# Upper parts of rotated rows and of later pages made on GpSimd instead of ScalarE, in a fused attention and FFN kernel

## The chip, the cores and the metric

The kernel runs on one core of a Trainium2 chip. The core has five engines, each with an instruction queue of its own: TensorE (PE, matmuls), VectorE (DVE), ScalarE (ACT), GpSimd (POOL) and SyncE (SP), which only issues DMAs here. Engines meet through semaphores. The metric is the device time of the whole program in microseconds (us).

## The reference

The reference is one transformer block with layer norms after each half, for x of shape (4, 512, 1024):

```python
def attn(x, wq, wk, wv, wo):             # 32 heads of 32, 8 key and value heads
    q, k, v = x @ wq, x @ wk, x @ wv
    q, k = rope(q), rope(k)              # pairs of columns rotated by position
    scores = q @ k.T / sqrt(32) + causal_mask
    return (softmax(scores) @ v) @ wo    # each k and v head serves 4 q heads

x = layernorm(x + attn(x, wq, wk, wv, wo))
gate = x @ (gate_t * gate_s[:, None]).T  # gate_t, up_t, down_t hold -1, 0, 1
up = x @ (up_t * up_s[:, None]).T        # 3584 hidden columns
hidden = silu(gate) * up
x = layernorm(x + hidden @ (down_t * down_s[:, None]).T)
```

All is float32 from outside.

## The kernel before

**Numbers.** Float32 operands are cut into an upper and a lower float16 part, and a product is three float16 matmuls (upper by upper, upper by lower, lower by upper). Two kinds of such cuts matter here.

*Pages.* x (16 pages), wq (8), wkv (4) and wo (8) come in as 36 pages of 128 partitions by 1024 float32, one DMA each (`page_load`, on SP). The upper part is made by `split_hi`, an activation Copy with a scale on ScalarE (line 1241; the first three pages are cut in halves, line 1239). The lower part is made by `split_lo` on VectorE (line 1384): page times scale minus upper part. The first 12 pages (`NFIRST`) have a buffer each, laid over tiles that are not used yet; the other 24 go through two buffers, `page0` and `page1`, so that a load waits for the split of the page two before it. These 24 are four pages of wq, the eight of wo and the twelve of x of the later three batches. The split of such an x page also waits until the former batch's q projection has used the place that it writes.

*Rotated rows.* Each q or k projection of 128 rows by 8 heads lands in PSUM (line 1070). VectorE multiplies it with cosines and sines (`rotate`, lines 1403 and 1405), GpSimd adds the two (`rope_add`, line 1631), ScalarE writes the upper float16 part twice into `stack_rows` (`nat_hi`, line 1257, 512 elements per partition), GpSimd writes the lower part (`nat_lo`, line 1638), and a transposing DMA on SP puts it into `q_stack` or `k_stack` (`stack`). There are 64 such rows for q and 16 for k. Two buffers each serve the rotated sum and the stack rows, so a `rotate` waits for `nat_hi` and `nat_lo` of two rows before.

**Attention.** It goes by 16 units (a batch and 8 heads). For a unit, PE first forms the scores by rows (`score_q`, line 1086); VectorE takes their maxima (`row_max`, lines 1414 to 1420), ScalarE exponentiates and sums them (`row_sum`, line 1280), and a few small steps make maximum plus logarithm of the sum (`ln_seed`, `ln_step`, `max_parts`, `max_tr`, `max_copy`, `max_rows`), which becomes three more rows of `q_stack`. Then PE forms the scores again by keys (`score_k`, line 1111), ScalarE exponentiates them (`exp`, line 1266), GpSimd zeroes the upper triangle (`causal`, line 1645), and PE multiplies with v (`pv`, line 1127). ScalarE and VectorE take the result out as two parts (`att_hi`, `att_lo`) and a DMA spills it. Projections of later units and output projections with wo (also line 1070) fill PE between these. Finished rows are added to x (`residual`), normed (`norm_stats`, `newton` on GpSimd, `norm`) and spilled, also as sums and differences in float16 (`x1_form`, `x1_hi`, `x1_lo`, `xF_store`).

**FFN.** It uses a scheme of seven products for each two by two blocks (line 1170, `product`). Its right operands, x1_forms, come back from DRAM by transposing DMAs (`xF_load`, line 1760); they lie over the projection weights and may start only when the last q projection is done. Weight pages are loaded (`w_load`), turned from int32 into float16 on ScalarE (`w_cast`, line 1319) and combined on VectorE (`w_form`). The down products (`down`, lines 1195 and 1211) are added up on VectorE (`acc`, line 1601). It makes two passes over the weights.

**What sets the order.** Every piece of work is put into a `Plan` with an engine, a rank (roughly its due time), a duration in us and the pieces it comes after. `Plan.close` is a list schedule: it steps through planned time, and on each engine the ready piece of the lowest rank goes next. The outcome is one fixed order for each engine; the program then issues exactly that, with semaphore waits. `SHIFTS` (line 232) adds a number to the rank of each kind of piece on its engine: a larger one makes that kind give way to others. `AT_ONCE` names pairs of kinds on one engine where the planner assumes no delay between the end of one and the start of the next. Each engine works strictly in its order, so an instruction that waits holds up all behind it.

Of the kernel before, what the change touches and what calls it, by code (L numbers as in the profile page):

```python
# [10 lines left out]
ACT = mybir.ActivationFunctionType  # L11

P = 128
# [8 lines left out]
UH = 8  # L22
# [192 lines left out]
def room_after(n):  # L215

    p, r = divmod(n, NF)
    if r > 2:
# [13 lines left out]
SHIFTS = {  # L232
    PE: {"down": 20, "max_tr": 17, "product": 45, "proj_out": -9, "proj_q": 126, "pv": 12, "score_k": 5, "score_q": 13},
    SC: {"exp": 328, "hid_hi": -4, "ln_exp": 32, "nat_hi": 381, "norm": 21, "row_sum": 156, "silu": 43, "split_hi": 54,
         "v_copy": -17, "w_cast": 233, "x1_hi": 8, "x1_store": 1},
    VE: {"acc": 3, "add_x1": -55, "att_lo": 195, "bound": 21, "d_form": 40, "ds_scale": 6, "hid_form": 9, "hid_lo": 37,
         "hidden": 55, "ln_seed": -2, "ln_step": 43, "max_copy": 218, "max_parts": 9, "norm_stats": 76, "residual": -4,
         "rotate": -64, "row_max": 53, "split_lo": 31, "sum": 14, "w_form": 60, "x1_lo": 18},
    PO: {"nat_lo": 7, "newton": -12, "rope_add": -45, "scale_row": 11, "x1_form": -2},
    SY: {"att_load": -3, "att_store": 58, "bound_load": -34, "bound_store": -16, "d_in": -20, "d_store": 64, "ds_load": -20,  # L240
         "last_x1": -2, "max_rows": -14, "out_store": 11, "page_load": -4, "row_load": -4, "stack": 11, "w_in": -30, "w_load": 19,
         "w_store": -24, "xF_load": 130, "xF_store": 3},
}


AT_ONCE = {("sum", "hidden"), ("hidden", "hid_form"), ("hid_form", "hid_form"), ("ln_step", "max_parts"), ("d_form", "d_form"), 
           ("residual", "norm_stats"), ("acc", "norm_stats"), ("x1_form", "x1_form"), ("ln_seed", "ln_step"), ("norm", "x1_store")}

# [87 lines left out]
def attention_plan(plan):  # L336
# [17 lines left out]
    for n, (what, b, j) in enumerate(loads):  # L354
        at = ranks[what, b, j]
        before = n - 2 if n >= NFIRST + 2 else NFIRST - 1 if what == "wo" else -1
        last = [loads[n - 1]] if n else []
        put(SY, at, .4, "page_load", what, b, j, moves=2 * FIRST_MOVES if n == 0 else FIRST_MOVES if n < NFIRST else PAGE_MOVES,
            after=[("split_lo", *loads[before])] if before >= 0 else [])
        put(SC, at, .95, "split_hi", what, b, j, after=[("page_load", what, b, j)] + [("split_hi", *w) for w in last] + (  # L360
            [("proj", "q", UNITS * b - 1, j, KD - 1)] if what == "x" and b else []))
        put(VE, at, 1.14, "split_lo", what, b, j, after=[("split_hi", what, b, j)] + [("split_lo", *w) for w in last])
# [26 lines left out]
    for n, (at, long, (what, w, t)) in enumerate(groups):  # L389
# [29 lines left out]
        put(PO, end + 1, .68, "rope_add", *one, after=[("rotate", *one)])  # L419
        put(SC, end + 2, .53, "nat_hi", *one, after=[("rope_add", *one)] + ([("nat_hi", *one_back)] if r else []) + ([("stack", *two_back)] if r > 1 else []))  # L420
        put(PO, end + 3, .68, "nat_lo", *one, after=[("nat_hi", *one)] + ([("nat_lo", *one_back)] if r else []))
# [299 lines left out]
def block_kernel(nc, xT, x, wq, wkv, wo, gateT, upT, downT, gate_s, up_s, down_s,  # L721
# [18 lines left out]
    with ctx:  # L740
        def sem(name):
            return ctx.enter_context(nc.semaphore(name))
# [79 lines left out]
        s_page = [sem(f"page_dma{i}") for i in range(2)]  # L822
        s_hi, s_lo = sem("split_hi"), sem("split_lo")
        s_half_hi, s_half_lo = sem("first_half_hi"), sem("first_half_lo")
# [40 lines left out]
        rot_n = {w: n for n, (k, w) in enumerate([p for p in plan.order[VE] if p[0] == "rotate"])}  # L865
        for engine, kind in ((PO, "rope_add"), (SC, "nat_hi"), (PO, "nat_lo"), (SY, "stack")):
            assert [w for k, w in plan.order[engine] if k == kind] == list(rot_n), kind
        splits = [w for k, w in plan.order[SY] if k == "page_load"]
        split_n = {w: n for n, w in enumerate(splits)}
        for engine, kind in ((SC, "split_hi"), (VE, "split_lo")):  # L870
            assert [w for k, w in plan.order[engine] if k == kind] == splits, kind
        trans = [(k, w) for k, w in plan.order[PE] if k == "max_tr" or (k == "score_q" and row_bank(*w) == TRANS)]
# [343 lines left out]
        def scalar_program(e):  # L1216
            on = Waits(e)
            e.dma_start(tab[:, :, :, :], rope).then_inc(s_tab, 16)
            for kind, which in plan.order[SC]:
                if kind == "split_hi":  # L1220
                    n = split_n[which]
                    if n == NFIRST - 2:
                        e.dma_start(idH[:, :], identH).then_inc(s_const, 16)
                        e.dma_start(idB[:, :], identB).then_inc(s_const, 16)
                        e.dma_start(cmask[:, :], causal).then_inc(s_const, 16)
                    elif n == NFIRST + 2:
                        e.dma_start(sg[:, :], gate_s).then_inc(s_scale, 16)
                        e.dma_start(su[:, :], up_s).then_inc(s_scale, 16)
                    src, arrived, times = page_of(n)
                    on.wait_ge(arrived, 16 * times)  # L1230
                    if which[0] == "wo":
                        on.wait_ge(s_lo, NFIRST)
                    if which[0] == "x" and which[1]:
                        on.wait_ge(s_proj, proj_n["q", which[1] * UNITS - 1, which[2]] + 1)
                    up = X_UP if which[0] == "x" else W_UP
# [6 lines left out]
                elif kind == "v_copy":  # L1242
# [5 lines left out]
                                         scale=PROJ_DOWN).then_inc(s_v, 1)  # L1248
                elif kind == "nat_hi":
                    r = rot_n[which]  # L1250
                    on.wait_ge(s_add, r + 1)
                    on.wait_ge(s_set, 1)
                    on.wait_ge(s_stack[r % NNAT], 16 * (r // NNAT))
                    rows = nat[:, r % NNAT, :, 0:STK].rearrange("p h (f c) -> p h f c", f=3)
                    fields = slice(0, 3, 2) if which[0] == "k" else slice(0, 2)
                    ta = ropeA[:, r % NNAT, :].rearrange("p (h c) -> p h c", h=UH)
                    nc.scalar.activation(rows[:, :, fields, :], ta.unsqueeze(2).broadcast_to([P, UH, 2, HD]),
                                         ACT.Copy).then_inc(s_nhi, 1)
                elif kind == "exp":
# [102 lines left out]
        def vector_program(e):  # L1362
# [7 lines left out]
            for kind, which in plan.order[VE]:  # L1370
                if kind == "split_lo":
# [5 lines left out]
                    if n < HALVED:  # L1377
# [4 lines left out]
                        hi, lo, whole = hi[:, mid:], lo[:, mid:], whole[:, mid:]  # L1382
                    on.wait_ge(s_hi, n + 1)
                    nc.vector.scalar_tensor_tensor(lo, whole, up, hi, ALU.mult, ALU.subtract).then_inc(s_lo, 1)
# [237 lines left out]
        def gpsimd_program(e):  # L1622
            on = Waits(e)
            nc.gpsimd.memset(nat[:, :, :, STK:P], MAX_ONE).then_inc(s_set, 1)
            for kind, which in plan.order[PO]:
                if kind == "rope_add":
# [3 lines left out]
                    to = ropeA[:, r % NNAT, :]  # L1630
                    nc.gpsimd.tensor_tensor(to, to, ropeB[:, r % 2, :], ALU.add).then_inc(s_add, 1)
                elif kind == "nat_lo":
                    r = rot_n[which]
# [49 lines left out]
        def sync_program(e):  # L1683
            on = Waits(e)
            for kind, which in plan.order[SY]:
                if kind == "page_load":
                    n = split_n[which]
                    dst, arrived, times = page_of(n)
                    if n >= NFIRST + 2:
                        on.wait_ge(s_hi, n - 1)  # L1690
                        on.wait_ge(s_lo, n - 1)
# [187 lines left out]
```

## Time and profile before

| what | us |
|---|---|
| median of 3 runs | 1781.22 |
| lowest and highest run | 1777.97 and 1781.43 |
| the profiled execution, its own time | 1779.99 |
| its span from first to last instruction | 1778.2 |

The profile is of one execution. Busy times are sums over an engine's instructions, in us of the span. PE has 9456 matmuls; they are pipelined and their ends are modelled, so small gaps between them can hide in its busy time. The chain of waits goes back from the last instruction, at each step to what released it, and gives each line its share of the stretch. The stage up to about 690 us is attention with its projections, the rest the FFN. TensorE's granted clock is 0.995 of full speed over the span.

### The profile page before, as it was taken

What the parts mean: (1) busy time and instruction counts of PE and PEld (TensorE: products, weight loads), DVE (VectorE), ACT (ScalarE), POOL (GpSimd) and SP (SyncE); (2) the same over time, 40 slices, a digit from 0 to 9 for tenths busy, and PEclk for the clock granted to TensorE, in tenths of its full rate; (3) what the DMA queues carried; (4) which work ended last, traced back from release to release, by engine and by line L of the source; (5) the groups of instructions that cost most, each with busy time, mean ns of one, the idle gap of its engine ahead of it and who ended that gap; (6) DMA issues with size and microseconds to landing.
All of it is one profiled execution on the core that took longest, in us unless ns stands there. A gap on an engine that the chain in (4) does not pass through costs nothing.

```text
span 1778.2 us, 26642 instructions
## 1 busy us (share of the span) xinstructions
PE 1711.6 (96%) x9456; PEld 824.8 (46%) x9456; DVE 1208.3 (68%) x2593; ACT 967.4 (54%) x2201; POOL 409.1 (23%) x782
## 2 busy tenths in 40 slices
PE   7979999999999999999999999999999999999998
PEld 4634555555455434444444444444444444443444
DVE  7776668478667744677877768746667666678456
ACT  6799989789978874472553543531323233231321
POOL 3324445445434442410000002103100000003113
PEclk9999999999999999999999999999999999999999
DMA  8543345335235698582653545658312112133202
GB/s 266 104 141 61 70 114 144 61 96 155 56 67 138 163 222 297 170 300 95 207 173 130 202 159 194 219 146 195 115 60 87 42 65 86 42 110 106 96 13 83
DMA packets 228004, 233.44 MB, mean 131 GB/s; under 512 B 183200, under 2 KB 183840, under 8 KB 227872
## 3 DMA queue, kind: packets, MB, share of 16 engines
q1 hardware_dynamic: 224704, 222.86, 42.9%
q10 hardware_dynamic: 3168, 8.88, 1.3%
q8 instruction: 75, 1.23, 0.3%
q14 instruction: 57, 0.47, 0.1%
HBM read 122.78 MB, written 72.88 MB: 110 GB/s over the span
## 4 chain that ended last, share of the span: by engine, by line
PE 71%; DVE 9%; DMA 8%; ACT 8%; issue 2%; POOL 1%; SPq 1%; DVEq 0%; ACTq 0%; POOLq 0%
PE bank L1170 31%; PE bank L1070 13%; PE bank L1211 12%; PE bank L1195 6%; ACT bank L1280 3%; PE bank L1111 3%; PE bank L1127 3%; PE bank L1086 2%; DMA w_page<-gateT 2%; DMA x_forms<-x_forms_spill 1%; ACT p_tiles L1266 1%; DMA w_page<-upT 1%; DMA q_stack<-max_rows 1%; DMA x_forms_spill<-x_parts 1%; DVE acc L1620 1%
## 5 line engine op out<-in xcount | busy, mean ns | idle before, releaser
L1170 PE MATMUL bank<-x_forms,weight_forms 128*128 128x512 f16 x3136 | 705.0, 379 | 7.8 <-DVE up_blocks L1566 4.1
L1170 PEld LDWEIGHTS bank<-x_forms,weight_forms 128*128 128x128 f16 x3136 | 305.4, 98 | 382.4 <-issue 9.9
L1280 ACT ACTIVATE bank<-bank,row_max 128x512 f32<-128x512 f32 (+3 forms) x512 | 265.3, 541 | 21.1 <-DVE row_max L1420 13.5
L1211 PE MATMUL bank<-down_forms 128*128 128x512 f16 x1120 | 267.4, 379 | 7.3 <-DVE acc L1601 7.3
L1420 DVE CUSTOM_DVE_ANT_0 bank<-bank,cmask 128x256 f32<-128x256 f32 (+2 forms) x384 | 206.6, 580 | 85.4 <-PE bank L1086 84.3
L1266 ACT ACTIVATE p_tiles<-bank 128x512 f32<-128x512 f32 (+1 forms) x352 | 194.7, 597 | 44.2 <-PE bank L1111 42.8
L1070 PE MATMUL bank<-wq_parts,xT_parts 128*128 128x256 f16 x1536 | 204.3, 276 | 8.6 <-DVE wq_parts L1380 8.0
L1601 DVE TENSOR_TENSOR acc<-bank,acc 128x512 f32<-128x512 f32 x248 | 167.2, 686 | 59.3 <-PE bank L1211 58.0
L1662 POOL TENSOR_TENSOR acc<-acc,down_forms 128x1024 f32<-128x1024 f32 x16 | 40.2, 2527 | 695.6 <-DVE acc L1601 695.6
L1645 POOL TENSOR_SCALAR_AFFINE_SELECT p_tiles<-p_tiles 128x128 f32<-128x128 f32 (+2 forms) x352 | 123.7, 358 | 231.2 <-ACT p_tiles L1266 227.9
L1211 PEld LDWEIGHTS bank<-down_forms 128*128 128x128 f16 x1120 | 108.7, 98 | 142.2 <-DVE acc L1601 13.1
L1070 PEld LDWEIGHTS bank<-wq_parts,xT_parts 128*128 128x128 f16 x1536 | 150.6, 99 | 49.8 <-DVE wq_parts L1380 8.0
L1070 PE MATMUL bank<-wo_parts,att_parts 128*128 128x512 f16 x672 | 163.6, 380 | 3.3 <-DMA att_parts<-att_spill 3.2
L1086 PE MATMUL bank<-k_stack,q_stack 96*128 96x512 f16 (+3 forms) x512 | 118.8, 302 | 16.9 <-ACT bank L1280 9.4
L1111 PE MATMUL bank<-q_stack,k_stack 99*128 99x512 f16 (+1 forms) x352 | 117.6, 365 | 12.5 <-DMA q_stack<-max_rows 6.0
L1360 ACT ACTIVATE down_forms<-gate_blocks 128x512 f16<-128x512 f32 x92 | 57.6, 626 | 131.6 <-DVE gate_blocks L1576 120.9
L1280 ACT ACTIVATION_READ_ACCUMULATOR bank<-bank,row_max 128x1 f32 x512 | 126.3, 247 | 0.0
L1566 DVE TENSOR_TENSOR up_blocks<-bank,up_blocks 128x512 f32<-128x512 f32 x84 | 57.8, 689 | 96.8 <-ACT up_blocks L1337 67.3
L1348 ACT ACTIVATE gate_blocks<-gate_blocks,gate_scale 128x512 f32<-128x512 f32 x84 | 60.3, 719 | 106.4 <-DVE gate_blocks L1566 106.4
L1195 PE MATMUL bank<-down_forms 128*128 128x512 f16 (+1 forms) x528 | 110.9, 373 | 0.0
L1070 PEld LDWEIGHTS bank<-wo_parts,att_parts 128*128 128x128 f16 x672 | 64.8, 98 | 75.2 <-issue 6.6
L1337 ACT ACTIVATE up_blocks<-bank 128x512 f32<-128x512 f32 x84 | 49.9, 594 | 88.9 <-PE bank L1170 88.7
(124 smaller groups left out, 1990.8 us busy)
## 6 DMA issues: line engine op xcount, KB each, us to landing
weight_forms_spill<-weight_forms SPq DMA_DIRECT2D x28, 896.0 KB, 5.6
weight_forms<-weight_forms_spill SPq DMA_DIRECT2D x28, 896.0 KB, 4.6
x_forms_spill<-x_parts SPq DMA_DIRECT2D x56, 256.0 KB, 2.5
w_page<-gateT SPq DMA_DIRECT2D x28, 512.0 KB, 4.7
w_page<-upT SPq DMA_DIRECT2D x28, 512.0 KB, 4.4
w_page<-downT SPq DMA_DIRECT2D x28, 512.0 KB, 4.9
att_spill<-att_made SPq DMA_DIRECT2D x32, 256.0 KB, 3.0
down_forms<-x_spill SPq DMA_DIRECT2D x16, 512.0 KB, 3.3
```

What stands on the lines that cost most here:

```text
L1070: t = nc.tensor.matmul(dst, left[:, a, k, rows], right[:, c, k, cols], start=k == 0 and m == 0, stop=last)
L1086: t = nc.tensor.matmul(to[:, h, :], qT[0:STK, u % QS, h0 + h, i * P:n], kT[0:STK, b % 2, kv_of(u, h0 + h), 0:n], start=h == 0, stop=h == R ...
L1111: nc.tensor.matmul(to, kT[0:STKM, b % 2, (u % UNITS) * UG + G, lo:lo + P], qT[0:STKM, u % QS, heads, lo:S], start=True, stop=True).then_in ...
L1170: t = nc.tensor.matmul(strassen[bank_set(use)][to][:, :], w_form[:, use % 4, A_FORMS[a_form], k * P:(k + 1) * P], xF[:, :, B_FORMS[b_form] ...
L1195: t = nc.tensor.matmul(to[:, 0:cols.stop - cols.start], hid_p[place_of(r)][:, k, a, i // 2 * P:(i // 2 + 1) * P], wd_p[place_of(r)][:, c, ...
L1211: t = nc.tensor.matmul(to[:, :], hid_f[r % NF % 3][:, HID_FORMS.index(a_form), a, pair * P:(pair + 1) * P], wd_f[r % NF % 3][:, DOWN_B[b_f ...
L1266: nc.scalar.activation(p32[j][:, h0:h0 + heads, :], bank[5 + m % 2][:, 0:heads * n].rearrange("p (h c) -> p h c", c=n), ACT.Exp, scale=SCO ...
L1280: nc.scalar.activation(scores, scores, ACT.Exp, scale=SCORE_DOWN if mask_added(i) else -1.0, bias=mx[:, u % 2, i, h:h + 1], accum_out=row_ ...
L1348: nc.scalar.activation(gate_t[:, k, :], src, ACT.Silu, scale=sg[:, 2 * (n % NF) + r:2 * (n % NF) + r + 1]).then_inc(s_silu, 1)
L1420: t = nc.vector.tensor_tensor_reduce(scores[:, h, :], scores[:, h, :], cmask[:, S - n:S], -SCORE_DOWN, -MASKED, ALU.add, ALU.min, mx[:, u ...
L1601: nc.vector.tensor_tensor(dst, got[:, :], dst, ALU.add).then_inc(s_acc, 1)
L1645: nc.gpsimd.affine_select(out=block, in_=block, compare_op=ALU.is_ge, fill=0.0, base=0, pattern=[[0, KEY_HEADS[j]], [1, P]], channel_multi ...
```

## The change

`split_hi` of the 24 later pages and all 80 `nat_hi` are issued on GpSimd instead of ScalarE, as a `tensor_scalar` multiplication and a `tensor_copy`. The later pages count on a semaphore of their own, `s_hi_late`, since two engines now make upper parts; the lower part waits for the one or the other. The wait on `s_hi` before a page load is dropped, as the wait on `s_lo` is kept. The two small loads of the FFN's scales are issued on ScalarE's queue with the last of the first 12 pages instead of two pages after them. In the planner the two pieces get GpSimd's durations (1.4 and 0.72), two pairs on GpSimd join `AT_ONCE`, and all of `SHIFTS` is set anew.

```diff
 SHIFTS = {
-    PE: {"down": 20, "max_tr": 17, "product": 45, "proj_out": -9, "proj_q": 126, "pv": 12, "score_k": 5, "score_q": 13},
-    SC: {"exp": 328, "hid_hi": -4, "ln_exp": 32, "nat_hi": 381, "norm": 21, "row_sum": 156, "silu": 43, "split_hi": 54,
-         "v_copy": -17, "w_cast": 233, "x1_hi": 8, "x1_store": 1},
-    VE: {"acc": 3, "add_x1": -55, "att_lo": 195, "bound": 21, "d_form": 40, "ds_scale": 6, "hid_form": 9, "hid_lo": 37,
-         "hidden": 55, "ln_seed": -2, "ln_step": 43, "max_copy": 218, "max_parts": 9, "norm_stats": 76, "residual": -4,
-         "rotate": -64, "row_max": 53, "split_lo": 31, "sum": 14, "w_form": 60, "x1_lo": 18},
-    PO: {"nat_lo": 7, "newton": -12, "rope_add": -45, "scale_row": 11, "x1_form": -2},
-    SY: {"att_load": -3, "att_store": 58, "bound_load": -34, "bound_store": -16, "d_in": -20, "d_store": 64, "ds_load": -20,
-         "last_x1": -2, "max_rows": -14, "out_store": 11, "page_load": -4, "row_load": -4, "stack": 11, "w_in": -30, "w_load": 19,
-         "w_store": -24, "xF_load": 130, "xF_store": 3},
+    PE: {"max_tr": 11, "product": 105, "proj_out": -2, "proj_q": 29, "pv": 28, "score_k": 9, "score_q": 16},
+    SC: {"att_hi": 5, "copy": -4, "exp": 357, "hid_hi": 1, "ln_exp": 56, "norm": 14, "row_sum": 75, "silu": 5, "split_hi": 1,
+         "v_copy": 18, "w_cast": 54, "x1_hi": -20, "x1_store": 19},
+    VE: {"acc": -180, "add_x1": -5, "att_lo": 8, "bound": -7, "d_form": 52, "ds_scale": -25, "hid_form": -6, "hid_lo": -40,
+         "hidden": 3, "ln_step": 6, "max_copy": 2, "max_parts": 30, "norm_stats": 7, "residual": 3, "rotate": 8, "row_max": 30,
+         "split_lo": 183, "sum": -87, "w_form": 81, "x1_lo": 69},
+    PO: {"causal": 11, "nat_hi": -9, "nat_lo": 18, "newton": 6, "rope_add": 3, "scale_row": -11, "split_hi": 60, "x1_form": 14},
+    SY: {"att_load": -84, "att_store": -10, "bound_load": -10, "bound_store": -2, "d_in": 19, "d_store": 9, "ds_load": 16,
+         "last_x1": 1, "max_rows": -147, "out_store": 14, "page_load": -5, "row_load": 4, "stack": -16, "w_in": -16, "w_load": -3,
+         "w_store": -4, "xF_load": -117, "xF_store": -35},
 }
...
-        put(SC, at, .95, "split_hi", what, b, j, after=[("page_load", what, b, j)] + [("split_hi", *w) for w in last] + (
+        put(SC if n < NFIRST else PO, at, .95 if n < NFIRST else 1.4, "split_hi", what, b, j, after=[("page_load", what, b, j)] + [("split_hi", *w) for w in last] + (
...
-        put(SC, end + 2, .53, "nat_hi", *one, after=[("rope_add", *one)] + ([("nat_hi", *one_back)] if r else []) + ([("stack", *two_back)] if r > 1 else []))
+        put(PO, end + 2, .72, "nat_hi", *one, after=[("rope_add", *one)] + ([("nat_hi", *one_back)] if r else []) + ([("stack", *two_back)] if r > 1 else []))
...
-                    on.wait_ge(s_hi, n + 1)
+                    if n < NFIRST:
+                        on.wait_ge(s_hi, n + 1)
+                    else:
+                        on.wait_ge(s_hi_late, n - NFIRST + 1)
...
+                elif kind == "nat_hi":
+                    r = rot_n[which]
+                    on.wait_ge(s_add, r + 1)
+                    on.wait_ge(s_set, 1)
+                    on.wait_ge(s_stack[r % NNAT], 16 * (r // NNAT))
...
+                    nc.gpsimd.tensor_copy(rows[:, :, fields, :], ta.unsqueeze(2).broadcast_to([P, UH, 2, HD])).then_inc(s_nhi, 1)
+                elif kind == "split_hi":
+                    n = split_n[which]
+                    src, arrived, times = page_of(n)
+                    on.wait_ge(arrived, 16 * times)
+                    if which[0] == "wo":
+                        on.wait_ge(s_lo, NFIRST)
+                    if which[0] == "x":
+                        on.wait_ge(s_proj, proj_n["q", which[1] * UNITS - 1, which[2]] + 1)
+                    nc.gpsimd.tensor_scalar(parts_of(*which)[0], as_parts(which[0], src), X_UP if which[0] == "x" else W_UP, None,
+                                            ALU.mult).then_inc(s_hi_late, 1)
...
-                        on.wait_ge(s_hi, n - 1)
                         on.wait_ge(s_lo, n - 1)
```

## Rows read from the trace of the kernel before

**Rows 1.** The page, part 1: busy us, share of the span, instructions.
```profile
PE 1711.6 (96%) x9456; PEld 824.8 (46%) x9456; DVE 1208.3 (68%) x2593; ACT 967.4 (54%) x2201; POOL 409.1 (23%) x782
```

**Rows 2.** Busy us by stretch: length, PE, PEld, DVE, ACT, POOL, clock, DMA, GB/s.
```profile
0.00:80.00 80.00, 65.51 (x447) 43.71 (x448) 58.56 (x142) 54.57 (x142) 26.09 (x34) 0.98 0.73 192
80.00:150.00 70.00, 58.94 (x422) 30.17 (x421) 54.81 (x167) 67.68 (x201) 26.54 (x56) 0.95 0.44 119
150.00:600.00 450.00, 440.52 (x3199) 238.48 (x3197) 307.29 (x943) 393.57 (x1149) 209.05 (x445) 1.00 0.41 98
600.00:700.00 100.00, 90.16 (x505) 36.34 (x503) 52.42 (x131) 66.99 (x153) 38.53 (x90) 0.98 0.96 247
700.00:1778.00 1078.00, 1056.49 (x4892) 476.13 (x4890) 735.23 (x1214) 384.61 (x563) 108.86 (x159) 1.00 0.39 131
```

**Rows 3.** Shares of the chain from 0:80, 80:150, 150:600 and 590:700, in this order.
```profile
by line: PE bank L1070 48.5%; PE bank L1086 6.3%; DMA page<-wo 6.2%; DMA page<-wq 6.2%; DMA p_tiles<-xT 5.3%; ACT bank L1280 5.3%; issue 4.0%; DMA q_stack<-stack_rows 3.8%; DVE wq_parts L1384 3.4%; ACT wq_parts L1241 1.3%; ACT wo_parts L124
...
by line: ACT bank L1280 30.4%; ACT p_tiles L1266 16.3%; PE bank L1070 6.9%; DMA page<-wo 6.4%; DMA page<-xT 5.9%; issue 4.5%; PE bank L1127 4.0%; DVE wo_parts L1384 3.7%; ACT stack_rows L1257 3.1%; ACT wo_parts L1241 3.0%; DVE bank L1420 2.
...
by line: PE bank L1070 39.0%; PE bank L1111 10.7%; PE bank L1127 10.4%; PE bank L1086 8.1%; ACT bank L1280 6.1%; issue 2.8%; DVE bank L1420 2.4%; DMA q_stack<-max_rows 2.3%; DMA x_forms_spill<-x_parts 1.8%; ACT p_tiles L1266 1.7%; DVE x_par
...
by line: PE bank L1070 21.6%; DMA x_forms<-x_forms_spill 20.1%; SPq L1760 8.0%; DMA att_parts<-att_spill 4.3%; DMA w_page<-gateT 4.2%; DMA q_stack<-max_rows 3.9%; DMA x_forms_spill<-x_parts 3.5%; PE bank L1170 3.3%; DMA w_page<-upT 3.2%; is
```

**Rows 4.** ACT's busy us (count) by stretch: line 1257 alone, then 1241 alone.
```profile
0.00:80.00 80.00, 8.75 (x14) 0.98 0.73 192
80.00:150.00 70.00, 5.60 (x8) 0.95 0.44 119
150.00:600.00 450.00, 38.20 (x57) 1.00 0.41 98
...
0.00:80.00 80.00, 18.44 (x19) 0.98 0.73 192
80.00:150.00 70.00, 9.53 (x9) 0.95 0.44 119
150.00:600.00 450.00, 8.51 (x8) 1.00 0.41 98
```

**Rows 5.** Pieces of the chain (start us, us); line 1241's group: busy, mean ns | idle.
```profile
97.49 1.05 ACT wo_parts L1241
133.07 0.52 ACT stack_rows L1257
...
L1241 ACT ACTIVATE xT_parts<-page 128x1024 f16<-128x1024 f32 x12 | 12.8, 1066 | 0.7 <-PE bank L1070 0.6
```

**Rows 6.** GpSimd's groups by shape (busy us, mean ns | idle); line 1631's ns min/median/max.
```profile
L1645 POOL TENSOR_SCALAR_AFFINE_SELECT p_tiles<-p_tiles 128x128 f32<-128x128 f32 x256 | 77.5, 307 | 165.3 <-ACT p_tiles L1266 162.7
L1645 POOL TENSOR_SCALAR_AFFINE_SELECT p_tiles<-p_tiles 128x512 f32<-128x512 f32 x32 | 20.4, 639 | 31.2 <-ACT p_tiles L1266 31.2
L1672 POOL TENSOR_TENSOR x_difference<-row 128x512 f32<-128x512 f32 x7 | 8.9, 1274 | 8.1 <-ACT row L1299 8.1
...
L1631 POOL TENSOR_TENSOR rope_cos<-rope_cos,rope_sin x80: 722/729/1749, 14.2 to 599.5; 128x256 f32<-128x256 f32 x80
```

**Rows 7.** Pieces of the chain from 20 to 100: page copies.
```profile
33.27 1.06 ACT wq_parts L1241
...
40.72 1.06 ACT wo_parts L1241
```

**Rows 8.** Waits over the span: total us, times, longest us.
```profile
POOL p_tiles L1645 <- ACT p_tiles L1266: 227.9, 206, 8.7
...
POOL stack_rows L1638 <- ACT stack_rows L1257: 33.7, 44, 3.4
...
PEld bank L1127 <- POOL p_tiles L1645: 8.0, 23, 0.4
```

**Rows 9.** The last q projection in the chain; SP's issues after it.
```profile
595.44 2.63 PE bank L1070 x24
...
598.14 2.62 SPq L1760 DMA_TRANSPOSE x_forms<-x_forms_spill  x2
```

More of the change, by code:

```diff
@@ L243 @@
+    PO: {"causal": 11, "nat_hi": -9, "nat_lo": 18, "newton": 6, "rope_add": 3, "scale_row": -11, "split_hi": 60, "x1_form": 14},
+    SY: {"att_load": -84, "att_store": -10, "bound_load": -10, "bound_store": -2, "d_in": 19, "d_store": 9, "ds_load": 16,
+         "last_x1": 1, "max_rows": -147, "out_store": 14, "page_load": -5, "row_load": 4, "stack": -16, "w_in": -16, "w_load": -3,
+         "w_store": -4, "xF_load": -117, "xF_store": -35},
 }
 AT_ONCE = {("sum", "hidden"), ("hidden", "hid_form"), ("hid_form", "hid_form"), ("ln_step", "max_parts"), ("d_form", "d_form"),
-           ("residual", "norm_stats"), ("acc", "norm_stats"), ("x1_form", "x1_form"), ("ln_seed", "ln_step"), ("norm", "x1_store")}
+           ("residual", "norm_stats"), ("acc", "norm_stats"), ("x1_form", "x1_form"), ("ln_seed", "ln_step"), ("norm", "x1_store"), ("rope_add", "nat_hi"), ("nat_hi", "nat_lo")}
@@ L822, in block_kernel @@
         s_page = [sem(f"page_dma{i}") for i in range(2)]
-        s_hi, s_lo = sem("split_hi"), sem("split_lo")
+        s_hi, s_hi_late, s_lo = sem("split_hi"), sem("split_hi_late"), sem("split_lo")
         s_half_hi, s_half_lo = sem("first_half_hi"), sem("first_half_lo")
@@ L865, in block_kernel @@
         rot_n = {w: n for n, (k, w) in enumerate([p for p in plan.order[VE] if p[0] == "rotate"])}
-        for engine, kind in ((PO, "rope_add"), (SC, "nat_hi"), (PO, "nat_lo"), (SY, "stack")):
+        for engine, kind in ((PO, "rope_add"), (PO, "nat_hi"), (PO, "nat_lo"), (SY, "stack")):
             assert [w for k, w in plan.order[engine] if k == kind] == list(rot_n), kind
@@ L869, in block_kernel @@
         split_n = {w: n for n, w in enumerate(splits)}
-        for engine, kind in ((SC, "split_hi"), (VE, "split_lo")):
-            assert [w for k, w in plan.order[engine] if k == kind] == splits, kind
+        assert [w for k, w in plan.order[VE] if k == "split_lo"] == splits
+        assert [w for e in (SC, PO) for k, w in plan.order[e] if k == "split_hi"] == splits
         trans = [(k, w) for k, w in plan.order[PE] if k == "max_tr" or (k == "score_q" and row_bank(*w) == TRANS)]
@@ L1225, in scalar_program @@
                         e.dma_start(cmask[:, :], causal).then_inc(s_const, 16)
-                    elif n == NFIRST + 2:
+                    elif n == NFIRST - 1:
                         e.dma_start(sg[:, :], gate_s).then_inc(s_scale, 16)
@@ L1230, in scalar_program @@
                     on.wait_ge(arrived, 16 * times)
[L1231 to L1234, printed above, removed]
                     up = X_UP if which[0] == "x" else W_UP
@@ L1248, in scalar_program @@
                                          scale=PROJ_DOWN).then_inc(s_v, 1)
[L1249 to L1258, printed above, removed]
                 elif kind == "exp":
@@ L1631, in gpsimd_program @@
                     nc.gpsimd.tensor_tensor(to, to, ropeB[:, r % 2, :], ALU.add).then_inc(s_add, 1)
+                elif kind == "nat_hi":
[3 more added lines that the diff above has]
+                    on.wait_ge(s_stack[r % NNAT], 16 * (r // NNAT))
+                    rows = nat[:, r % NNAT, :, 0:STK].rearrange("p h (f c) -> p h f c", f=3)
+                    fields = slice(0, 3, 2) if which[0] == "k" else slice(0, 2)
+                    ta = ropeA[:, r % NNAT, :].rearrange("p (h c) -> p h c", h=UH)
+                    nc.gpsimd.tensor_copy(rows[:, :, fields, :], ta.unsqueeze(2).broadcast_to([P, UH, 2, HD])).then_inc(s_nhi, 1)
[9 more added lines that the diff above has]
+                                            ALU.mult).then_inc(s_hi_late, 1)
                 elif kind == "nat_lo":
```

## The prediction
> **What bounds the kernel now.** I read the page first: TensorE (PE) is busy for 1711.6 of 1778.2 us [rows 1]. Then the busy times by stage [rows 2] (the first number after each stretch is its length, then PE, PE's weight loads, VectorE, ScalarE, GpSimd). They show the only places where PE has idle time to give: 80.00 - 65.51 = 14.5 us up to 80, 70.00 - 58.94 = 11.1 us from 80 to 150, 450.00 - 440.52 = 9.5 us from 150 to 600, 100.00 - 90.16 = 9.8 us from 600 to 700, and 1078.00 - 1056.49 = 21.5 us in the whole FFN after that. Idle before 700 is 44.9 us, and that bounds from above what this change can bring in attention, give or take a few us that a pipelined engine's busy time hides. Third, the chain of waits cut into the same stretches [rows 3]. It tells what the idle time is made of. From 80 to 150 it runs mostly over ScalarE: 30.4 + 16.3 + 3.1 + 3.0 = 53% (row sums, exponentials, the copies of rotated rows and of pages); ScalarE is busy there for 67.68 of 70 us. From 150 to 600 it runs over PE's own matmuls, ScalarE holds only 6.1 + 1.7 = 8%. Up to 80 it is PE and pages, ScalarE about 5.3 + 1.3 = 7%. Around 600 to 700 it is transposing DMAs (20.1 + 8.0%). So the kernel is PE-bound, with a ScalarE-bound piece of some 70 us at the start of the steady attention and a DMA-bound piece at its end.
>
> **The change, part by part.** Two kinds of instruction leave ScalarE, and a full set of planner shifts changes beside them.
>
> *What leaves ScalarE.* 80 copies of rotated rows (nat_hi, line 1257) and 24 of the 36 page copies (split_hi, line 1241; 17 + 7 late ones by the counts below). By stretch [rows 4]: copies of rows 14, 8 and 57 (one is left after 600), page copies 19, 9 and 8. Of the first 19, twelve belong to the first pages and stay, so 7, 9 and 8 move. On the chain a row copy holds ScalarE for 0.52 us and a page copy for 1.05 us [rows 5] (their spans are longer, since one begins before the last has drained). Moved work: 14 x 0.52 + 7 x 1.05 = 14.6 us up to 80; 8 x 0.52 + 9 x 1.05 = 13.6 us from 80 to 150; 57 x 0.52 + 8 x 1.05 = 38.0 us after. A us taken off ScalarE is worth a us only while the chain is on ScalarE, so I weigh each by that share: 14.6 x 0.07 = 1.0, 13.6 x 0.53 = 7.2, 38.0 x 0.08 = 3.0. Sum: 11.2 us saved. Ends: at nothing, if PE's idle time has another cause beside it; at 1.0 + 11.1 + 9.5 = 21.6 us, if all of PE's idle time from 80 to 600 goes. What comes late next in 80 to 150 is PE itself (58.94 busy of 70) and the page loads, 6.4 + 5.9% of that chain.
>
> *What GpSimd pays.* The trace has no plain copy on GpSimd. From below: the causal select, one input, takes 307 ns at 128 elements a partition and 639 ns at 512 [rows 6]: 0.865 ns an element, so 0.64 us for a row copy of 512 and 1.08 us for a page of 1024. From above: a subtraction of two 512-element inputs takes 1274 ns [rows 6], so 1.27 and, doubled, 2.55 us. A copy has one input, and the select is the nearer row: I take 0.65 and 1.3 us. Less than the select's time is possible too (it computes a mask), but hidden, as GpSimd is no bound: it is busy 26.54 of 70 and 209.05 of 450 us [rows 2], and gets 8 x 0.65 + 9 x 1.3 = 17 us and 57 x 0.65 + 8 x 1.3 = 47 us more: 62% and 57%. At the upper price it is 80% and 67%.
>
> The Trainium skill says the like: "GPSIMD Engine Reference", section 3.1, puts a one-input loop at 1.03 cycles an element and 1.2 GHz, an estimate of 0.44 us plus dispatch for 512 elements, and two inputs at about 2.5 cycles. By its one-input figure the sum below would be some 0.5 us better.
>
> *Pages on the path.* In the chain a page copy follows its load directly (33.27 and 40.72 us [rows 7]), then VectorE makes the lower part and only then is the next load issued. Five page copies stand so before 105 us. Each becomes 1.3 instead of 1.06 us: 5 x 0.24 = +1.2 us; with the ends +0.1 and 5 x 1.49 = +7.5. The dropped wait on the upper part before a load costs and gives nothing: the lower part that is still waited for is made from it. The scale loads issued earlier on ScalarE's queue are small, and their reader is a reduction on VectorE much later: nothing.
>
> *What queues behind them.* GpSimd works in order. Behind a copy stand causal selects, and pv (line 1127) waits for them; today that wait is short, 8.0 us in 23 waits [rows 8]. From 80 to 700 the moved work fills 66 x 0.65 + 17 x 1.3 = 65 us, a tenth of the time, so a pv's last select meets a moved copy one time in ten and waits some 0.4 us: 64 x 0.1 x 0.4 = 2.6 us, of which PE feels about half, having other matmuls ready: +1.3 us. At the upper price the share is 66 x 1.27 + 17 x 2.55 = 127 us, a fifth, and the mean wait 0.85 us: 64 x 0.2 x 0.85 = +11 us. Below: 0. A page copy of x now waits on GpSimd until the former batch's projection is done; on ScalarE these 12 copies waited only 0.6 us for PE [rows 5], so I put it at nothing here. The other direction is a gain: the lower part of a row waited 33.7 us in 44 waits for ScalarE's copy [rows 8], which is now the instruction ahead on the same engine. The stack DMA comes earlier by that, but PE waits for stacks hardly at all after 80, so nothing.
>
> *The shifts.* They change the fixed order on every engine. Most of it lies beside PE's own work, and I see no sign for either direction; two edits I can place. Projections of q were far behind score matmuls in rank (126 against 5 and 13) and come near them (29 against 9 and 16). The transposing loads of x1_forms may start only after the last q projection: it ends at 598.07 and the first load is issued at 598.14 us [rows 9]. After that DMAs are busy 96% [rows 2], and the chain holds 28% of 110 us in these loads [rows 3]. With projections and those loads (130 to -117) ranked earlier, this block starts earlier and overlaps more. Bounds: 0 to the 9.8 us idle there; I take 3 us, near the low end because the chain also holds other DMAs there. In the FFN products fall behind down products (105 against 0, before 45 against 20). PE has 21.5 us idle in it, partly at its very end; I take 0, with 4 us to either side, a fifth of that idle time.
>
> **The sum.** -11.2 + 1.2 + 1.3 - 3.0 = -11.7 us. The profiled execution took 1779.99 us for a span of 1778.2, 1.2 us under the median 1781.22; I count the difference from the median: 1781.2 - 11.7 = 1769.5 us.
>
> **Rivals.**
> *A, nothing that can be measured (within 0.2%, 3.6 us).* PE's idle time from 80 to 150 is the ramp of attention (few score stacks ready) and not ScalarE's load. For it: after 150 PE is 98% busy with ScalarE at 393.57 of 450 us. Against it: the 53% of ScalarE in the chain. It gives -1.0 + 1.2 + 1.3 = +1.5, about 1783 us.
>
> *B, slower: GpSimd's queue becomes the late one.* Place: selects behind page and row copies. A rotated sum on GpSimd took 722 ns at best, 729 in the median and 1749 at worst [rows 6], so something beside it more than doubles it at times. If the copies cost their upper price, the pages add 7.5 us and the selects 11 us. Twelve page copies of x wait for a projection in a queue that also holds the selects; if half of them stand 1.3 us (half of a q projection) that is 8 us. -11.2 - 3.0 + 7.5 + 11 + 8 = +12.3, and I take a milder mix, +8: 1789 us. It decides from the point where each of the 64 pvs is late by (11.2 + 3.0) / 64 = 0.22 us. For it: order in one queue is fixed by a planner that has to guess. Against it: GpSimd stays under 70% busy, and its selects wait 227.9 us for exponentials already [rows 8].
>
> The Trainium skill has the mechanism: "GPSIMD Engine Reference", section 8, says that GpSimd shares its SBUF interfaces with VectorE and contends with instructions that have two SBUF inputs, as the lower part has. The trace's 1749 ns agrees with it.
>
> *C, much faster.* The relief lets projections and scores run ahead, and the end of attention starts its DMAs earlier. Half of the idle 44.9 us before 700, and 3 us of the FFN: -25, 1756 us. For it: ScalarE was 87% busy from 150 to 600, so nothing queued there could ever catch up. Against it: the chain of that stretch is PE.
>
> **Chances.** The forecast 0.46, A 0.14, B 0.25, C 0.15. A comparison of this kernel tells about 0.2%, 3.6 us, from no change. Forecast and C are faster: 0.61. Same 0.14, slower 0.25. The likeliest case alone spans 1761 to 1777 us; the range 1753 to 1789 adds C's and B's side.
>
> **What would show it.** Right: from 80 to 150 PE idle falls from 11 to about 4 us and the chain leaves ScalarE; row copies on GpSimd take 0.6 to 0.7 us and pages 1.1 to 1.5; pv's wait for selects stays under 12 us; the first x1_forms load is well before 598 us. Wrong: row copies over 1 us, pv waiting over 20 us for selects, or rotations waiting for GpSimd; or PE's idle time in the FFN changing by more than 5 us, which would mean that the new order and not the move decides.

## The result and the profile after

The changed kernel takes 1792.07 us in the median of 4 runs (1789.74 to 1795.44), the kernel before 1781.33 us beside it. The ratio is 1.0050 with a 95% interval of 1.0026 to 1.0075: slower by 8.9 us by the ratio (5 to 13 us by its interval) and by 10.7 us by the medians, where 1769.5 us was forecast with a range up to 1789. The profiled execution is the slowest of the four, 1795.44 us with a span of 1793.7 us.

The page of the changed kernel, part 1 [rows 1], shows that the work was moved: ScalarE lost 57.8 us of busy time, GpSimd gained 127.6 us.

```profile
PE 1717.7 (96%) x9456; PEld 829.7 (46%) x9456; DVE 1221.6 (68%) x2593; ACT 909.6 (51%) x2097; POOL 536.7 (30%) x886
```

The busy times by stage, with the columns of [rows 2]:

```profile
0.00:80.00 80.00, 61.54 (x398) 39.05 (x399) 57.35 (x129) 38.17 (x109) 56.99 (x51) 0.96 0.64 184
80.00:150.00 70.00, 62.53 (x479) 35.20 (x478) 60.81 (x176) 59.29 (x195) 63.88 (x80) 1.00 0.48 106
150.00:600.00 450.00, 431.01 (x3092) 233.70 (x3090) 307.11 (x927) 348.17 (x1056) 258.32 (x487) 0.99 0.41 98
600.00:700.00 100.00, 90.86 (x539) 38.59 (x538) 54.01 (x143) 68.79 (x168) 46.95 (x108) 0.95 0.90 210
700.00:1778.00 1078.00, 1064.19 (x4907) 478.42 (x4905) 732.31 (x1195) 391.92 (x573) 107.84 (x154) 1.00 0.40 134
```

Against [rows 2], PE's idle time is 18.5 us instead of 14.5 up to 80, 7.5 instead of 11.1 from 80 to 150, 19.0 instead of 9.5 from 150 to 600, and 9.1 instead of 9.8 from 600 to 700. By 700 us PE has issued 4508 matmuls instead of 4573. GpSimd is now the fullest helper from 80 to 150, with 63.88 of 70 us. Of the 15.5 us between the two spans, 9.4 are idle time of PE; the other 6.1 are busy time (1717.7 instead of 1711.6) for the same 9456 matmuls, at a mean granted clock of 0.990 instead of 0.995.

The chain of waits, its shares from 0 to 80, 80 to 150 and 150 to 600 in this order [rows 3]:

```profile
by line: issue 28.7%; PE bank L1070 17.9%; POOL wq_parts L1638 10.4%; POOL rope_cos L1620 6.5%; POOL stack_rows L1646 6.3%; POOL stack_rows L1629 5.9%; POOL wo_parts L1638 4.7%; PE bank L1086 4.5%; DVE bank L1409 3.8%; ACT bank L1266 3.1%; 
...
by line: POOL xT_parts L1638 15.6%; POOL p_tiles L1653 10.7%; issue 10.3%; PE bank L1070 9.0%; POOL wo_parts L1638 8.0%; ACT bank L1266 5.7%; PE bank L1111 4.2%; POOL rope_cos L1620 4.1%; DMA q_stack<-max_rows 4.1%; PE bank L1086 3.8%; POOL
...
by line: PE bank L1070 36.1%; PE bank L1127 8.7%; PE bank L1111 7.5%; PE bank L1086 6.5%; ACT bank L1266 6.2%; issue 4.8%; POOL xT_parts L1638 3.1%; ACT p_tiles L1252 2.7%; POOL p_tiles L1653 2.2%; POOL stack_rows L1629 1.5%; DVE bank L1409
```

From 80 to 150 ScalarE's row sums, 30.4% of the chain before, are down to 5.7% (they are line 1266 in the changed kernel). GpSimd took the place: pages 15.6 + 8.0%, selects 10.7%. The groups of GpSimd by shape say why (busy us, mean ns of one):

```profile
L1629 POOL CAST stack_rows<-rope_cos 128x512 f16<-128x512 f32 x80 | 54.0, 676 | 3.4 <-DMA q_stack<-stack_rows 1.1 <-DMA k_stack<-stack_rows 0.4
...
L1638 POOL TENSOR_SCALAR xT_parts<-page 128x1024 f16<-128x1024 f32 x12 | 33.4, 2786 | 1.9 <-PE bank L1070 1.9
...
L1638 POOL TENSOR_SCALAR wo_parts<-page 128x1024 f16<-128x1024 f32 x8 | 24.1, 3012 | 0.0
...
L1638 POOL TENSOR_SCALAR wq_parts<-page 128x1024 f16<-128x1024 f32 x4 | 13.0, 3261 | 0.0
```

A row copy costs 676 ns, nearly the 0.65 us of the forecast. A page costs 2.8 to 3.3 us, above even the upper bound of 2.55 us: 33.4 + 24.1 + 13.0 = 70.5 us for 24 pages. The waits for a select [rows 8] and for GpSimd's pages:

```profile
PEld bank L1127 <- POOL p_tiles L1653: 19.9, 23, 2.7
...
PE bank L1127 <- POOL p_tiles L1653: 10.3, 8, 2.4
...
DVE wo_parts L1373 <- POOL wo_parts L1638: 8.4, 4, 2.7
DVE xT_parts L1373 <- POOL xT_parts L1638: 8.3, 6, 3.2
```

The two rows of pv (line 1127) are not to be added: the matmuls' 10.3 us lie inside the 19.9 us that their weight loads wait. So pv's weight loads wait 19.9 us for selects instead of 8.0, its matmuls 10.3 us instead of not at all, and the longest wait is 2.7 instead of 0.4 us, the length of a page. Seven of the eight waits of its matmuls begin during a page on GpSimd or within 2 us after one. A piece of the chain shows one such place, where a page of x, the three instructions of a rotated row, another page and the selects stand in line and pv comes after them:

```profile
440.81 2.80 POOL xT_parts L1638
443.60 0.70 POOL rope_cos L1620
444.31 0.06 issue
444.36 1.48 POOL stack_rows L1629
...
445.93 1.00 POOL stack_rows L1646
446.93 2.24 POOL xT_parts L1638
449.17 0.49 issue
449.66 1.39 POOL p_tiles L1653 x3
451.05 0.04 issue
451.10 1.51 PE bank L1127 x16
```

### The profile page after: what moved, and what is told of

Same layout as the page of the kernel before. It is cut to its first block, busy times and chain, and to the rows that moved or that the text cites. A ratio compares the mean times of both kernels' runs of the same rounds, so it can differ in the third digit from the quotient of the medians.

```text
span 1793.7 us, 26556 instructions
## 1 busy us (share of the span) xinstructions
PE 1717.7 (96%) x9456; PEld 829.7 (46%) x9456; DVE 1221.6 (68%) x2593; ACT 909.6 (51%) x2097; POOL 536.7 (30%) x886
## 4 chain that ended last, share of the span: by engine, by line
PE 71%; DVE 7%; POOL 7%; DMA 6%; ACT 4%; issue 4%; SPq 1%; DVEq 0%; ACTq 0%; POOLq 0%
PE bank L1170 33%; PE bank L1070 13%; PE bank L1211 12%; PE bank L1195 6%; PE bank L1127 2%; PE bank L1111 2%; ACT bank L1266 2%; PE bank L1086 2%; DMA x_forms<-x_forms_spill 2%; POOL xT_parts L1638 1%; DMA x_forms_spill<-x_parts 1%; POOL p_tiles L1653 1%; ACT p_tiles L1252 1%; POOL rope_cos L1620 1%; POOL stack_rows L1629 1%
## 5 line engine op out<-in xcount | busy, mean ns | idle before, releaser
L1266 ACT ACTIVATE bank<-bank,row_max 128x512 f32<-128x512 f32 (+3 forms) x512 | 260.9, 520 | 71.0 <-DVE row_max L1409 51.7
L1252 ACT ACTIVATE p_tiles<-bank 128x512 f32<-128x512 f32 (+1 forms) x352 | 190.3, 580 | 65.1 <-PE bank L1111 62.2
L1070 PE MATMUL bank<-wq_parts,xT_parts 128*128 128x256 f16 x1536 | 210.7, 275 | 8.0 <-DVE wq_parts L1366 8.0
L1653 POOL TENSOR_SCALAR_AFFINE_SELECT p_tiles<-p_tiles 128x128 f32<-128x128 f32 (+2 forms) x352 | 132.2, 384 | 167.1 <-ACT p_tiles L1252 164.7
L1555 DVE TENSOR_TENSOR up_blocks<-bank,up_blocks 128x512 f32<-128x512 f32 x84 | 57.8, 689 | 98.1 <-ACT up_blocks L1323 63.7
L1266 ACT ACTIVATION_READ_ACCUMULATOR bank<-bank,row_max 128x1 f32 x512 | 114.5, 224 | 0.0
L1660 POOL TENSOR_SCALAR rstd<-rstd 128x1 f32<-128x1 f32 x93 | 37.2, 400 | 242.4 <-DVE rstd L1470 236.2
L1070 PE MATMUL bank<-wkv_parts,xT_parts 128*128 128x512 f16 x384 | 99.5, 392 | 4.7 <-DVE rope_sin L1394 4.7
```

The source lines that it names most:

```text
L1070: t = nc.tensor.matmul(dst, left[:, a, k, rows], right[:, c, k, cols], start=k == 0 and m == 0, stop=last)
L1252: nc.scalar.activation(p32[j][:, h0:h0 + heads, :], bank[5 + m % 2][:, 0:heads * n].rearrange("p (h c) -> p h c", c=n), ACT.Exp, scale=SCO ...
L1266: nc.scalar.activation(scores, scores, ACT.Exp, scale=SCORE_DOWN if mask_added(i) else -1.0, bias=mx[:, u % 2, i, h:h + 1], accum_out=row_ ...
L1653: nc.gpsimd.affine_select(out=block, in_=block, compare_op=ALU.is_ge, fill=0.0, base=0, pattern=[[0, KEY_HEADS[j]], [1, P]], channel_multi ...
```

## The experiments

Theory 1 says that the price of a page on GpSimd is the loss; theory 2, the new order; theory 3, the row copies. Ratios are to the kernel before; 0.001 is 1.8 us. Edits are against the changed kernel, where nothing else is said.

**cast.** The page without its multiplication, order unchanged on every engine:

```diff
-X_UP, W_UP = 2.0 ** 6, 2.0 ** 8
+X_UP, W_UP = 1.0, 1.0
...
-                    nc.gpsimd.tensor_scalar(parts_of(*which)[0], as_parts(which[0], src), X_UP if which[0] == "x" else W_UP, None,
-                                            ALU.mult).then_inc(s_hi_late, 1)
+                    nc.gpsimd.tensor_copy(parts_of(*which)[0], as_parts(which[0], src)).then_inc(s_hi_late, 1)
```

> The changed kernel in the same order on every engine, but both scales X_UP and W_UP are 1 and the late page is a plain copy to float16 on GpSimd. Theory 1 (the page multiplication of 2.77 us in GpSimd's queue is the loss): the copy takes about 1.1 to 1.3 us, pv's wait for selects falls from 30 us to about 10, and the time is 1772 to 1780 us. Theory 2 (the new order is the loss): the copy gets shorter and the time stays within 4 us of 1792. Theory 3 (the row copies and their contention with VectorE are the loss): also above 1787.

Measured: 1762.68 us, ratio 0.9905 (0.9888 to 0.9921). This beats both kernels, and by more than theory 1 asked. Its groups of pages, its first three stages, and pv's wait:

```profile
L1638 POOL CAST xT_parts<-page 128x1024 f16<-128x1024 f32 x12 | 12.9, 1074 | 2.6 <-PE bank L1070 2.6
L1638 POOL CAST wo_parts<-page 128x1024 f16<-128x1024 f32 x8 | 9.9, 1243 | 1.5 <-DMA page<-wo 1.5
L1638 POOL CAST wq_parts<-page 128x1024 f16<-128x1024 f32 x4 | 6.1, 1531 | 0.0
```

```profile
0.00:80.00 80.00, 68.23 (x484) 44.84 (x485) 64.94 (x161) 46.96 (x139) 52.66 (x66) 1.00 0.74 194
80.00:150.00 70.00, 68.54 (x506) 36.15 (x503) 62.58 (x179) 66.85 (x212) 50.69 (x89) 1.00 0.58 139
150.00:600.00 450.00, 438.82 (x3173) 238.35 (x3171) 316.44 (x955) 358.89 (x1092) 251.38 (x500) 1.00 0.44 103
```

```profile
PEld bank L1127 <- POOL p_tiles L1652: 6.3, 16, 1.6
```

The 24 pages cost 28.9 instead of 70.5 us. PE's idle time is 11.8, 1.5 and 11.2 us, and pv waits 6.3 us. Of 41.6 us taken off GpSimd, 0.0145 x 1781 = 26 us came off the time, give or take some 5 us by the two intervals. The order and the row copies are the same in both kernels, so theories 2 and 3 fall as the cause of this part. The scales of 1 also change the numbers that all engines work on; that this alone gains nothing is argued from cast_old_shifts and op_prices below, and has no run of its own.

**nat_only, split_only, shifts_only.** The new shifts with one or both kinds of copy back on ScalarE (with the durations and waits that they had there):

```diff
-        put(SC if n < NFIRST else PO, at, .95 if n < NFIRST else 1.4, "split_hi", what, b, j, ...
+        put(SC, at, .95, "split_hi", what, b, j, ...
```

```diff
-        put(PO, end + 2, .72, "nat_hi", *one, ...
+        put(SC, end + 2, .53, "nat_hi", *one, ...
```

> The new shifts, row copies on GpSimd, all page copies back on ScalarE with the planner's old duration for them. Theory 1: 1770 to 1778 us, faster than before. Theory 2: above 1787. Theory 3: above 1787.

> The new shifts, late pages on GpSimd, row copies back on ScalarE. Theory 1: 1790 to 1800 us. Theory 2: near 1792. Theory 3: 1776 to 1784 us.

> The new shifts alone, both kinds of copy on ScalarE as before. Theory 1: within 4 us of the kernel before, 1781. Theory 2: 1792 or more. Theory 3: within 4 us of 1781.

Measured: nat_only (first edit) 1.0009 (0.9990 to 1.0027), 1782.43 us; split_only (second edit) 1.0245 (1.0230 to 1.0260), 1823.99 us; shifts_only (both) 1.0161 (1.0146 to 1.0176), 1808.90 us. Theory 3 expected the last two near 1781 us, and both are far slower. But theory 1 alone missed all three: shifts_only was to be like before and is 28 us slower, nat_only was to be faster and is not, split_only was to end at 1800 at most. Theory 2 missed nat_only and split_only. The new shifts are bad for the old placement, with one reservation. The planner adds no shift to a kind that a set doesn't name for its engine, and the new set has no `nat_hi` on ScalarE. There the row copies run with shift 0, where the old set has 381. Whether the other new shifts or this one missing number makes shifts_only and split_only slow was not tried.

**move_old_shifts, nat_old_shifts, cast_old_shifts, old_both.** The other half of the table, with the `SHIFTS` of before put in place of the new ones; copies as in the changed kernel, in nat_only, in cast, and both on ScalarE. The set of before names neither kind on GpSimd, so a moved kind has shift 0 there.

> Both copies on GpSimd (multiplication, 2.77 us a page), but the shifts of the kernel before; the two moved kinds get shift 0 there. If the set of shifts belongs to a placement (as the first four runs say), this is slower than the changed kernel: 1800 us or more. If the loss is the page price alone, whatever the order: 1788 to 1796.

> Shifts of the kernel before, only the row copies on GpSimd. Relief of ScalarE helps by itself: 1770 to 1778 us. The order must be fitted to a placement before relief shows: 1782 to 1800.

> As the plain-copy kernel (scales 1, both copies on GpSimd), with the shifts of the kernel before. If the gain of 18 us over the kernel before is the move of work at a fair price: 1762 to 1772. If it is the joint fit of shifts and placement: 1778 or more.

> Both copies on ScalarE and the old shifts: only the small edits of the change are left (scale loads issued earlier, a second semaphore, the dropped wait, AT_ONCE). Every theory: within 3 us of the kernel before.

Measured: move_old_shifts 1.0136 (1.0105 to 1.0168), nat_old_shifts 1.0005 (0.9989 to 1.0020), cast_old_shifts 0.9996 (0.9983 to 1.0008), old_both 0.9994 (0.9981 to 1.0007). So the small edits are worth nothing, and so, with the old shifts, is the move itself at the plain copy's price. With them the multiplication costs 1.0136 - 0.9996 = 0.0140, 25 us, as much as with the new ones.

**cast_split_only.** The plain-copy kernel with the row copies back on ScalarE.

> New shifts, late pages as plain copies on GpSimd, row copies back on ScalarE. If the row copies make most of the relief: 1790 us or more. If the pages do: 1765 to 1775.

Measured: 1.0125 (1.0110 to 1.0140), 1801.52 us. With the new shifts, moving the row copies too carries the time from there to 0.9905. How much of this is relief of ScalarE, and how much the missing shift of the row copies there, is open: all three runs with new shifts and row copies on ScalarE are slow.

| on GpSimd | shifts of before | new shifts |
|---|---|---|
| nothing | 0.9994 | 1.0161 |
| row copies | 1.0005 | 1.0009 |
| pages, multiplied | not run | 1.0245 |
| pages, plain copy | not run | 1.0125 |
| both, multiplied | 1.0136 | 1.0050 (the change) |
| both, plain copy | 0.9996 | 0.9905 |

**cost28 and cast_cost11.** One number of the planner, in the changed kernel and in the plain-copy kernel:

```diff
-        put(SC if n < NFIRST else PO, at, .95 if n < NFIRST else 1.4, "split_hi", ...
+        put(SC if n < NFIRST else PO, at, .95 if n < NFIRST else 2.8, "split_hi", ...
```

> The changed kernel, with 2.8 instead of 1.4 us told to the planner for a late page on GpSimd; nothing else. If the loss is that the order was laid out for a page half as long: 1775 to 1786 us. If it is the time in the queue itself: 1788 to 1800.

> The plain-copy kernel (scales 1, both copies on GpSimd, new shifts) with 1.1 instead of 1.4 us told to the planner for a page. The measured copy takes 1.04 us. If nearer durations help whatever the shifts: 1755 to 1762 us. If the shifts were fitted to the order that 1.4 gives: the same or slower, 1762 to 1775.

Measured: cost28 1.0004 (0.9992 to 1.0016), 1782.64 us; cast_cost11 (1.1 in place of 1.4) 0.9967 (0.9954 to 0.9980), 1774.34 us. Told the true price, the planner wins back 0.0046, some 8 us of the 26. That looks as if part of the loss were an order laid out for pages half as long. But the truer 1.1 in the plain-copy kernel made it 11 us slower. One duration alters the whole order, and an effect of this size can't be put down to the truer price by one run.

**op_prices.** The kernel before with five instructions in GpSimd's idle first microseconds, on a tile of ones:

```diff
...
+            for step, (to, op) in enumerate(((half, "mult"), (half, "copy"), (low, "mult"), (half, "mult"), (half, "copy"))):
+                on.wait_ge(s_try, step + 1)
+                if op == "mult":
+                    nc.gpsimd.tensor_scalar(to, low, 1.0, None, ALU.mult).then_inc(s_try, 1)
+                else:
+                    nc.gpsimd.tensor_copy(to, low).then_inc(s_try, 1)
...
```

> The kernel before with five more GpSimd instructions at its start, where GpSimd is idle, on 128x512 elements: multiplication by a constant float32 to float16, plain copy float32 to float16, multiplication float32 to float32, and the first two again. If the multiplication itself is dear on GpSimd: about 1.4 us against 0.6 for the copy, in both output types. If the output type is what costs: the float32 multiplication near 0.6 us. If contention with VectorE is what costs: the two passes differ widely.

One execution, GpSimd in order of time (start us, us):

```profile
1.86 1.53 POOL L1630 TENSOR_SCALAR x_parts<-x_difference 128x512 f16<-128x512 f32 x1
3.45 0.61 POOL L1632 CAST x_parts<-x_difference 128x512 f16<-128x512 f32 x1
4.15 1.50 POOL L1630 TENSOR_SCALAR x_difference<-x_difference 128x512 f32<-128x512 f32 x1
5.73 1.49 POOL L1630 TENSOR_SCALAR x_parts<-x_difference 128x512 f16<-128x512 f32 x1
7.29 0.67 POOL L1632 CAST x_parts<-x_difference 128x512 f16<-128x512 f32 x1
```

The multiplication takes 2.5 times the copy, in both output types. VectorE's first instruction begins at 5.78 us in this run, so the first three ran without it, and the other two cost nearly the same. It is the operation that is dear, not its output type or its neighbour, and not the data, as all five work on ones. Contention is in the changed kernel too: its 4 pages of 3.7 us all ran beside VectorE's lower parts of pages (line 1373), and the 20 of 2.8 us mostly did not. That is some 1 us on each of four pages, 4 of the 70.5 us.

## Why the prediction was wrong

**The step that failed** is the page's price in "What GpSimd pays". It took 1.3 us, from the causal select, "the nearer row". The measured 2.94 us on average lies above both ends. The select has one input and so has the multiplication, but input count was the wrong thing to go by. The copy of a row, priced from the same row, was right: 0.65 forecast, 0.68 measured. With 2.94 and 0.68 us in the prediction's own formulas the pages on the path cost 5 x 1.88 = 9.4 us. The moved work then fills 66 x 0.68 + 17 x 2.94 = 95 of 620 us, and a select that meets it waits 0.93 us on average (half the length of what it meets, weighted by the time that each kind fills), 64 x 0.15 x 0.93 = 9 us. The sum becomes -11.2 + 9.4 + 9 - 3.0 = +4 us (an estimate). This one price turns its sign, and the runs agree: the multiplication costs 25 us, and without it the change is faster by 0.0095. Two other terms were off and partly cancel: ScalarE's relief (-11.2 us forecast, nothing with the old shifts) and the shifts (-3 us forecast, -15 us measured).

The Trainium skill led the same way. "GPSIMD Engine Reference", section 3.1, gives 1.03 cycles an element for bodies of at most two operations an element; at 1.2 GHz that is an estimate of 0.88 us for 1024, without dispatch. The plain copy agrees: 0.61 us for 512 and 1.03 us for 1024 at best are 0.82 ns an element, against 0.86 by the page. The multiplication by a constant takes 2.77 us at best, and there the trace decides. By this figure the term of the pages alone would have been up to 5 x (1.3 - 0.88) = 2.1 us lower, not the 0.5 us that the prediction gives.

**Pages on the path.** Forecast +1.2 us, up to +7.5. PE's idle time up to 80 rose by 4.0 us, near the middle of these ends, and the plain copy brings it 2.7 us below before.

**What queues behind.** Forecast +1.3 us with an upper end of +11. The wait of pv's weight loads for selects rose by 11.9 us and that of its matmuls by 10.3 us. So the upper end was about right, and the middle failed by the page's price and by the half that PE was to feel. The whole price of the multiplication, pages and queue together, is 25 to 26 us, against the 7.5 + 11 of the upper ends; the rest of it is not placed. The load of GpSimd had a slip too: at the upper price it is (26.54 + 33.1) / 70 = 85% from 80 to 150 and not 80%, and it was 91%.

**ScalarE's relief.** Forecast -11.2 us, of which -7.2 from 80 to 150. There PE's idle time did fall by 3.6 us, and in the plain-copy kernel by 9.6 us, so the ScalarE-bound piece was real. But with the old shifts the move at the plain copy's price gives 0.9996. The profile of cast_old_shifts gives back late what it gains early (PE's busy us from 80, 150 and 600 on, clock, DMA, GB/s):

```profile
80.00:150.00 70.00, 65.15 (x462) 0.95 0.53 124
150.00:600.00 450.00, 435.64 (x3147) 1.00 0.42 98
600.00:700.00 100.00, 88.17 (x485) 0.97 0.95 245
```

Idle time is 4.8 instead of 11.1 us, but then 14.4 instead of 9.5 and 11.8 instead of 9.8. A share of the chain times the moved work says what could be gained, not that a fixed order will take it.

**The shifts.** Forecast -3 us, "no sign for either direction". Measured with both copies moved: 1.0050 - 1.0136 = -0.0086, 15 us of gain, and -0.0091 at the plain copy's price. With only the row copies moved they gain nothing (1.0009 against 1.0005). With nothing moved they lose 0.0167, 30 us, with the reservation above. The mechanism that I named is not refuted by the first x1_forms load starting later than before, at 607.9 us instead of 598.1, since the page's price came in between. With the placement held fixed the load does start earlier with the new shifts, by 11.1 us with pages multiplied and by 19.1 us with plain copies (move_old_shifts, changed kernel, cast_old_shifts, cast):

```profile
619.03 2.63 SPq L1767 DMA_TRANSPOSE x_forms<-x_forms_spill  x2
607.90 3.62 SPq L1767 DMA_TRANSPOSE x_forms<-x_forms_spill  x2
595.39 2.63 SPq L1766 DMA_TRANSPOSE x_forms<-x_forms_spill  x2
576.33 3.26 SPq L1766 DMA_TRANSPOSE x_forms<-x_forms_spill  x2
```

The time fell by 15 and 16 us beside it. So the direction was right and the size, 3 us, too small; whether the early loads make the gain or only mark an earlier end of attention isn't shown. Which of the shifts carries it was not tried. The FFN, put at 0 with 4 us to either side, is alike: of the 1050 us after 700 PE is busy for 1036.35 before and 1036.19 after.

**The rivals.** B came true, with its place (selects behind page and row copies) and a page price above its own. That its size (1789 us forecast) is near is in part luck: it counts -11.2 us of relief, which with the old shifts is nothing, and -3 us for shifts that gain 15. Its point of decision, 0.22 us for each of the 64 pvs, was not passed by the selects alone: 11.9 / 64 = 0.19 us. Its 8 us for pages of x that hold up the queue did not come: GpSimd waited only 1.9 us for PE before these 12 pages. Contention with VectorE, which it named for the dear copies, is a small part; the op alone costs this much. In numbers, the change is +25 us for the multiplication, -15 us for the new shifts in the new placement, and about nothing for the rest.

## What to carry to other kernels

Price a moved operation by the same operation on the same engine, and if the trace has none, keep the range open to a multiple of the nearest row; a copy and a multiplication by a constant differ 2.5 times on this one. Where a scale can be absorbed elsewhere, drop it and move a plain copy: here it turned +0.5% into -0.95%. What dropping these two scales does to the error of the result was not measured. A planner's shifts belong to one placement: compare a move only with shifts fitted to both sides, with an entry for each moved kind on both engines, and expect some 10 us from a change of a single duration.

## What the runs showed of the hardware

On GpSimd a conversion of 512 float32 to float16 takes 0.61 us and of 1024 1.03 us at best; a multiplication by a constant takes 1.50 and 2.77 us, more than a subtraction of two tensors (1.27 us for 512 [rows 6]). A constant scale is thus dearer there than a second input. Some of GpSimd's instructions take about a us more than the rest of their kind: pages 3.7 us and not 2.77, row copies 1.5 to 1.8 and not 0.61. The trace of the changed kernel points at VectorE. Its 4 pages of 3.7 us, its 5 row copies of 1.48 us and more and its 7 sums of rotated rows of 1.6 us and more (0.72 at best) all ran beside line 1373, a VectorE instruction with two inputs in SBUF. Of the shorter ones, 2 of 20 pages, 5 of 75 row copies and 4 of 73 sums did. No run takes that instruction away, so this is a strong coincidence and not a test.
